# A four-layer graph network on one core: the opening loads put in order, the split of the edge network's first weight moved to 12 partitions, and some copies moved to ScalarE

## What is computed

```python
x = _layernorm(x + L0(x, src, dst, ...))              # attention over edges
x = _layernorm(x + relu((x + segment_sum(x[src], dst)) @ W))
e_h = silu(edge_attr @ edge_W1 + edge_b1)             # 53125 x 4 -> 128
e_w = sigmoid(e_h @ edge_W2 + edge_b2)                # one weight for each edge
x_agg = silu(x[src] @ agg_W + agg_b) * e_w            # L2, then update and norm
x = _layernorm(x + L3(x, edge_index, edge_type, ...))
```

## Time and profile before

| | us |
|---|---|
| median of 3 runs | 1098.27 (1097.43 to 1101.11) |
| the profiled execution: time | 1098.61 |
| the profiled execution: span | 1096.8 |
| PE busy in the span | 1009.4 (92%) |
| DVE busy | 907.4 (83%) |
| ACT busy | 722.1 (66%) |
| POOL busy | 217.8 (20%) |

### The profile page before, as it was taken

How to read it: one execution, slowest core, us unless ns; L and a number is a source line. 1 busy time by engine, 2 the same in 40 slices (tenths; PEclk the granted TensorE clock), 3 DMA queues, 4 the chain that set the end, 5 groups by cost and what they waited for, 6 DMA issues and landing times.

```text
span 1096.8 us, 28220 instructions
## 1 busy us (share of the span) xinstructions
PE 1009.4 (92%) x10463; PEld 865.8 (79%) x10463; DVE 907.4 (83%) x2226; ACT 722.1 (66%) x1559; POOL 217.8 (20%) x260
## 2 busy tenths in 40 slices
PE   3797979699999999995999999779999999989997
PEld 3343557599999999994677787759999999976765
DVE  6775999988998989988999999878787888766754
ACT  3466765555545555457899999567677776776554
POOL 4401340000000000000000000226676667610000
PEclk9899999899999999996999999889999999999999
DMA  6000020344444445410543344235444444357463
GB/s 158 1 1 1 4 68 3 110 147 149 165 128 157 157 139 168 135 64 21 168 130 128 126 124 127 75 113 141 126 142 138 121 138 133 116 188 237 145 171 116
DMA packets 79198, 128.27 MB, mean 117 GB/s; under 512 B 11147, under 2 KB 53206, under 8 KB 78828
## 3 DMA queue, kind: packets, MB, share of 16 engines
q1 hardware_dynamic: 73577, 115.20, 33.5%
q0 software_dynamic: 5056, 10.36, 3.8%
q10 hardware_dynamic: 426, 0.85, 0.3%
HBM read 101.50 MB, written 24.88 MB: 115 GB/s over the span
## 4 chain that ended last, share of the span: by engine, by line
PE 76%; DVE 12%; ACT 6%; issue 3%; DMA 1%; POOL 0%; POOLq 0%; SPq 0%; DVEq 0%; ACTq 0%
PE PS L2424 14%; PE PS L2618 14%; PE PS L2412 11%; PE PS L2601 8%; PE PS L2704 6%; PE PS L2529 5%; PE PS L2497 2%; PE PS L2250 2%; PE PS L2504 2%; PE PS L2263 2%; DVE vo L1592 2%; DVE ring L1588 2%; PE PS L2327 2%; ACT ring L1221 1%; ACT X L1160 1%
## 5 line engine op out<-in xcount | busy, mean ns | idle before, releaser
L1084 ACT CAST vo<-XT 128x768 f32<-128x768 bf16 (+1 forms) x218 | 180.3, 827 | 136.7 <-PE PS L2618 64.1
L920 POOL DMA_INDIRECT XT<-tab,ring x158 | 160.6, 1016 | 112.0 <-PE PS L2618 60.8
L2424 PE MATMUL PS<-vo 128*128 128x133 f32 x1300 | 175.9, 284 | 1.0 <-DVE vo L1694 1.0
L2424 PEld LDWEIGHTS PS<-vo 128*128 128x128 f32 x1300 | 157.2, 191 | 1.1 <-issue 1.1
L2412 PE MATMUL PS<-kp,ring 128*128 128x132 bf16 x1950 | 146.1, 220 | 3.3 <-DVE ring L1562 1.8
L2618 PE MATMUL PS<-vo 128*128 128x128 f32 x984 | 132.8, 279 | 0.0
L2412 PEld LDWEIGHTS PS<-kp,ring 128*128 128x128 bf16 x1950 | 125.3, 97 | 5.5 <-DVE ring L1562 1.9
L1570 DVE TENSOR_TENSOR XT<-iotab,XT 128x768 bf16<-128x768 bf16 (+1 forms) x218 | 119.8, 550 | 2.5 <-ACT XT L1077 2.5
L2618 PEld LDWEIGHTS PS<-vo 128*128 128x128 f32 x984 | 118.9, 191 | 3.0 <-issue 2.4
L2414 PE MATMUL PS<-SDP,ring 128*128 128x12 bf16 x650 | 110.0, 169 | 0.0
L1562 DVE TENSOR_SCALAR ring<-ring,pcolm 128x1664 bf16<-128x1664 bf16 x146 | 91.0, 651 | 19.1 <-PE PS L2601 15.5
(11 more groups left out here) (345 smaller groups left out, 2134.2 us busy)
## 6 DMA issues: line engine op xcount, KB each, us to landing
ring<-rows_d SPq DMA_DIRECT2D x146, 416.0 KB, 4.7
adj_d<-ring SPq DMA_DIRECT2D x100, 128.0 KB, 1.7
adj_d<-ring SPq DMA_DIRECT2D x75, 96.0 KB, 1.6
ring<-adj_d SPq DMA_DIRECT2D x11, 640.0 KB, 4.2
vo<-adj_d SPq DMA_DIRECT2D x9, 640.0 KB, 4.2
vo<-adj_d SPq DMA_DIRECT2D x8, 480.0 KB, 3.9
ring<-adj_d SPq DMA_DIRECT2D x7, 480.0 KB, 4.4
XT<-tab,ring POOLq DMA_INDIRECT x158
```

The lines of the kernel that those rows point to most:

```text
L920: G.indirect_dma_start(far_rows[:, f % FBUF, :], None, tab[2], bass.IndirectOffsetOnAxis(ap=far_row[:, t:t + 1], axis=0)).then_inc(far_in[ ...
L1084: C.copy(ohd[:, k % 3, 0:n, :], ohb[:, k % 3, 0:n, :]).then_inc(hots_wide, 1)
L2424: T.matmul(bank(6 + b % 2)[:, 0:VW], ohd[:, k % 3, i, :], vals[:, k % 3, i, :], start=j == 0, stop=j == JN - 1).then_inc(scattered, 1)
```

## The change

The loads of the opening are put in order by waits: the attribute loads on ScalarE's queue wait for the edge list to land (`edges_in`), and the node rows on SyncE's queue wait for the attributes (`attr_in`). `edge_W1` is loaded three times onto 12 partitions and `edge_b1` broadcast beside it (`W12`). VectorE splits these 12 x 256 numbers into three parts, choosing by partition, ahead of its wait for the edge list; TensorE's product with `S` then spreads parts that are final, and ScalarE copies the result from `bank(4)` to `We1b`. The selectors `psel` fall away, small ones in `pgrp` come. ScalarE also takes over the copy of columns 80 to 96 of `attrS`, and does one small Silu early. GpSimd clears only the spare columns of `SLc`, and makes three small iotas in place of one.

```diff
@@ -374,9 +374,13 @@
         hv = big[:, 6864:7376].rearrange("p (k f) -> p k f", k=4)
-        We1 = big[:, 6864:6864 + GE]
-        we1a = big[:, 7376:7376 + GE // 2].bitcast(bf16)
-        we1c = big[:, 7632:7632 + GE // 2].bitcast(bf16)
+        W12 = T0f[0:12, 0:2 * F]
+        W12a = T0f[0:12, 2 * F:3 * F].bitcast(bf16)
+        W12c = T0f[0:12, 3 * F:4 * F].bitcast(bf16)
+        W12p = T0f[0:12, 4 * F:6 * F]
+        S = T0f[0:12, 6 * F:10 * F].rearrange("p (u r) -> p u r", u=U)
+        code = T0f[0:12, 10 * F:10 * F + ATT]
+        pgrp = T0f[0:12, 11 * F:11 * F + 8]
         We1b = sb("We1b", [P, U * F], bf16)
@@ -384,13 +388,8 @@
...
-        S = sb("S", [4, U, P])
-        S1 = sb("S1", [1, P])
-        psel = sb("psel", [P, 3])
+        code_i = sb("code_i", [12, ATT], i32)
+        S1 = sb("S1", [3, P])
@@ -676,6 +675,7 @@
             sp.wait_ge(padded, 4)
+            sp.wait_ge(attr_in, 16 * (len(ROWS) + (REM > 0)))
             sp.dma_start(X[:, 0:HNB, :], ins["x"][0:HNB * P, :].rearrange("(b p) f -> p b f", p=P)).then_inc(x_in, 16)
@@ -823,7 +823,8 @@
             G.iota(iota_i[:, :], pattern=[[1, P]], base=0, channel_multiplier=0).then_inc(iotas, 1)
-            G.iota(m16_i[:, :], pattern=[[0, P // 16], [1, 16]], base=0, channel_multiplier=0).then_inc(iotas, 1)
+            for part, (c0, c1) in enumerate(((0, 48), (48, 80), (80, 96))):
+                G.iota(code_i[:, c0:c1], pattern=[[0, (c1 - c0) // 16], [1, 16]], base=16 * part, channel_multiplier=0).then_inc(iotas, 1)
             G.iota(pcol_i[:, :], pattern=[[0, 1]], base=0, channel_multiplier=1).then_inc(iotas, 1)
@@ -831,9 +832,9 @@
             G.memset(onesb[:, :], 1.0).then_inc(pool_consts, 1)
-            G.memset(SLc[:, :, :, :], 0.0).then_inc(pool_consts, 1)
+            G.memset(SLc[:, :, :, 4 * (NB % BANKS) + 3:BP:4], 0.0).then_inc(pool_consts, 1)
             G.memset(attrS[:, :, ATT:ATW], 1.0).then_inc(pool_consts, 1)
             G.tensor_copy(IJ[:, :], iota_i[:, 1:JN + 1]).then_inc(pool_consts, 1)
@@ -965,8 +966,10 @@
 
-            act.dma_start(eW1[:, :], ins["edge_W1"]).then_inc(we1_in, 16)
-            act.dma_start(eb1[:, :], ins["edge_b1"].rearrange("(o f) -> o f", o=1)).then_inc(we1_in, 16)
+            for part in range(3):
+                act.dma_start(W12[4 * part:4 * part + 4, 0:F], ins["edge_W1"]).then_inc(we1_in, 16)
+            act.dma_start(W12[:, F:2 * F], ins["edge_b1"].rearrange("(o f) -> o f", o=1).to_broadcast([12, F])).then_inc(we1_in, 16)
+            act.wait_ge(edges_in, 16 * 3 * (len(ROWS) + (REM > 0)))
             for n, (r0, r1) in enumerate(ROWS):
@@ -979,6 +982,8 @@
 
+            act.wait_ge(consts, 1)
+            C.activation(okr[:, :], pcol[:, :], ACT.Silu)
             for k in range(2):
@@ -989,8 +994,12 @@
             C.copy(attrS[:, :, 0:16], attrE).then_inc(part_act, 1)
+            act.wait_ge(part_act, 1)
+            C.copy(attrS[:, :, 80:96], attrS[:, :, 0:16]).then_inc(part_act, 1)
             act.wait_ge(part_dve, 1)
             C.copy(attrS[:, :, 16:32], attrE).then_inc(part_act, 1)
+            act.wait_ge(we1_mm, 1)
+            C.copy(We1b[:, :], bank(4)).then_inc(we1_ready, 1)
             def heads_copy(k):
@@ -1405,13 +1414,32 @@
             V.memset(X[:, NB - 1, :], 0.0).then_inc(padded, 1)
...
              dve.sem_inc(consts, 1)
+
+            link(V.tensor_scalar(pgrp[:, 0:1], pcol[0:12, :], 4.0, None, ALU.is_ge))
+            link(V.scalar_tensor_tensor(pgrp[:, 1:2], pcol[0:12, :], 8.0, pgrp[:, 0:1], ALU.is_ge, ALU.add))
+            loose(V.scalar_tensor_tensor(pgrp[:, 2:3], pgrp[:, 1:2], 12.0, pcol[0:12, :], ALU.mult, ALU.add))
+            for part in range(3):
+                loose(V.tensor_scalar(pgrp[:, 3 + part:4 + part], pgrp[:, 1:2], float(part), None, ALU.is_equal))
+            loose(V.tensor_copy(code, code_i[:, :]))
+            loose(V.memset(S, 0.0))
+            loose(V.memset(S1[:, :], 0.0))
+            dve.wait_ge(we1_in, 64)
+            link(V.tensor_copy(W12a, W12))
+            link(V.tensor_tensor(W12, W12, W12a, ALU.subtract))
+            link(V.tensor_copy(W12c, W12))
+            link(V.tensor_tensor(W12, W12, W12c, ALU.subtract))
+            for c0, sel in ((0, pgrp[:, 3:6]), (F, ident[0:12, 0:3])):
+                cs = slice(c0, c0 + F)
+                link(V.tensor_scalar(W12p[:, cs], W12[:, cs], sel[:, 2:3], None, ALU.mult))
+                link(V.scalar_tensor_tensor(W12p[:, cs], W12c[:, cs], sel[:, 1:2], W12p[:, cs], ALU.mult, ALU.add))
+                loose(V.scalar_tensor_tensor(W12p[:, cs], W12a[:, cs], sel[:, 0:1], W12p[:, cs], ALU.mult, ALU.add))
 
@@ -1421,16 +1449,13 @@
 
-            loose(V.memset(S[:, :, :], 0.0))
-            loose(V.memset(S1[:, :], 0.0))
             loose(V.memset(eps[:, :], LN_EPS))
-            loose(V.tensor_copy(m16[:, :], m16_i[:, :]))
             loose(V.tensor_copy(identb[:, :], ident[:, :]))
...
             settle()
-            loose(V.memset(S1[:, ATT:ATK], 1.0))
+            loose(V.tensor_copy(S1[:, ATT:ATK], ident[0:3, 0:3]))
             for u in range(U):
-                loose(V.tensor_scalar(S[:, u, 0:ATT], m16[:, 0:ATT], -4.0 * u, pcol[0:4, 0:1], ALU.add, ALU.is_equal))
+                loose(V.tensor_scalar(S[:, u, 0:ATT], code, -4.0 * u, pgrp[:, 2:3], ALU.add, ALU.is_equal))
             settle()
@@ -1452,15 +1477,8 @@
             loose(V.tensor_scalar(pcolm[:, :], pcol[:, :], -float(P), None, ALU.add))
-            for k, n in enumerate((48, 80, 96)):
-                loose(V.tensor_scalar(psel[:, k:k + 1], pcol[:, :], float(n), None, ALU.is_lt))
             settle()
-            loose(V.scalar_tensor_tensor(TRI[:, :], ident[:, :], RANK0, TRI[:, :], ALU.mult, ALU.add))
-            link(V.tensor_tensor(psel[:, 2:3], psel[:, 2:3], psel[:, 1:2], ALU.subtract))
-            link(V.tensor_tensor(psel[:, 1:2], psel[:, 1:2], psel[:, 0:1], ALU.subtract))
-            for k in range(3):
-                loose(V.scalar_tensor_tensor(psel[:, k:k + 1], pcol[:, :], float(ATT + k), psel[:, k:k + 1], ALU.is_equal, ALU.add))
-            settle()
+            link(V.scalar_tensor_tensor(TRI[:, :], ident[:, :], RANK0, TRI[:, :], ALU.mult, ALU.add))
             dve.sem_inc(consts, 1)
@@ -1509,20 +1527,9 @@
             rank_hots(0)
-            dve.wait_ge(we1_mm, 1)
-            link(V.tensor_copy(We1, bank(4)))
-            link(V.tensor_copy(we1a, We1))
-            link(V.tensor_tensor(We1, We1, we1a, ALU.subtract))
-            link(V.tensor_copy(we1c, We1))
-            link(V.tensor_tensor(We1, We1, we1c, ALU.subtract))
-            link(V.tensor_scalar(We1b[:, :], we1a, psel[:, 0:1], None, ALU.mult))
-            link(V.scalar_tensor_tensor(We1b[:, :], we1c, psel[:, 1:2], We1b[:, :], ALU.mult, ALU.add))
-            link(V.scalar_tensor_tensor(We1b[:, :], We1, psel[:, 2:3], We1b[:, :], ALU.mult, ALU.add))
-            dve.sem_inc(we1_ready, 1)
-            dve.wait_ge(part_act, 2)
+            dve.wait_ge(part_act, 3)
             dve.wait_ge(part_dve, 1)
             loose(V.tensor_copy(attrS[:, :, 48:80], attrS[:, :, 0:32]))
-            loose(V.tensor_copy(attrS[:, :, 80:96], attrS[:, :, 0:16]))
             settle()
@@ -2228,11 +2235,10 @@
             pe.wait_ge(consts, 2)
-            pe.wait_ge(we1_in, 32)
             pe.wait_ge(base_ready, 1)
             for u in range(U):
-                T.matmul(bank(4)[:, u * F:(u + 1) * F], S[:, u, :], eW1[:, :], start=True, stop=False)
-                o = T.matmul(bank(4)[:, u * F:(u + 1) * F], S1[:, :], eb1[:, :], start=False, stop=True)
+                T.matmul(bank(4)[:, u * F:(u + 1) * F], S[:, u, :], W12p[:, 0:F], start=True, stop=False)
+                o = T.matmul(bank(4)[:, u * F:(u + 1) * F], S1[:, :], W12p[0:3, F:2 * F], start=False, stop=True)
             o.then_inc(we1_mm, 1)
@@ -2310,7 +2316,7 @@
-                    pe.wait_ge(part_act, 2)
+                    pe.wait_ge(part_act, 3)
```

8 lines of the change are left out of this document (2 added, 6 removed).

## The result

The changed kernel took 1092.02 us (median of 5 runs, 1088.86 to 1094.81), against 1098.27 for the kernel before (5 runs, 1097.43 to 1101.11). The ratio is 0.9938 with an interval of 0.9913 to 0.9964: 6.2 us less, where 9.6 were forecast. The profiled execution took 1093.46 with a span of 1091.6, against 1096.8 for the span of before.

A forecast was written before the change was run, and what follows sets the result against it. TensorE bounds the kernel as a whole, but the opening waits on a load and then VectorE. Front 2.1, block 5.7 and clock 1.8 sum to 9.6: 1098.6 - 9.6 = 1089.0 us, range 1085.5 to 1094.0.

The forecast's parts named there:

- The term of the front: Opening up to the edge list's cast: cast starts at 8.8 in place of 10.93, 2.1 us earlier.
- a clock that falls anyway: Rival: remaining TensorE idle time still makes the clock fall, leaving a 7.2 us gain, 1091.4 us; chance 0.20.
- late small loads: Rival: small weight loads land late and VectorE stalls ahead of the cast, gain 6.5, 1092.1 us; chance 0.10.
- three signs of being wrong: Attributes landing after 13, clock at 0.50 behind attr_transposed(0), or mixed stage's 9.6 us gain missing at the end.
- The edge list's landing: Opening: loaded without the attributes beside it, the edge list lands near 7.0 us.
- The attributes' landing: Opening: issued after the edge list, 830 KB takes 3.5 us plus 2.2 for the way, landing at 12.7.
- The rival by late attributes: Slower: attributes loaded behind the edge list hold up their strand; decides at a landing of 22.4; chance 0.02.
- The split ahead of the cast: VectorE's weight split on 12 partitions before the edge list's cast: 3.7 us from 5.1, so the cast starts at 8.8.
- The bounds of -1.0 and 3.9: Limits on the front's 2.1 us: 3.9 if only the landing counts, -1.0 if the small loads land at 8.2.
- The work between the one-hot planes: VectorE work removed between rank_hots(0) and rank_hots(1): rank_sums(3) gains 5.7 us, between 5.1 and 6.0, limited by TensorE.
- The clock: TensorE's idle stretch before rank_sums(3) goes, so its clock no longer falls behind it: 1.8 us, up to 2.4.
- rival of a gain given back: Rival: stages behind 98 us idle and lose clock anew, 7.2 of 9.6 lost, 1096.2 us; chance 0.06.

The follow-up runs named there:

- small_loads_last: Changed kernel with the four layer L0 tensors, edge_W2 and edge_b2 loaded behind the attributes: 1089.74 us, ratio 0.992 to the kernel before.
- clears_late: Changed kernel with GpSimd's clearings behind the first one held until the edge list is cast: 1092.87 us, one run.
- no_load_waits: Changed kernel without the two waits that order the attribute and node-row loads: 1092.07 us, ratio 0.9942 to the kernel before.
- copy_back: Changed kernel with the copy of columns 80 to 96 of attrS back on VectorE, off ScalarE: 1092.71 us, one run.
- all_three: Changed kernel with six small loads behind the attributes, GpSimd's clearings held until the edge cast, and the split behind the edge list's fields: 1087.74 us, ratio 0.9899.
- no_early_silu: Changed kernel without the small early Silu on ScalarE, so the table loads at the first real Silu: 1091.24 us, one run.

## Why the prediction came out 3 us too low

**The direction and two of the three terms** were right: the idle stretch of TensorE is gone, the clock holds in the mixed stage, and all that stands before the placement moves with them. The term of the front was not. Of 9.6 us, 8.1 are there at the placement, and the 1092.0 us lie in the range, 3.0 above the forecast. That owes something to luck: the 2.9 us given back behind the placement (below) could as well have been more or less. Two rivals give such a number (1091.4 by a clock that falls anyway, 1092.1 by late small loads), but neither is what happened: the clock held, and the small loads of the weight were there when VectorE asked (4.99). Of the prediction's own three signs of being wrong, two came: the attributes landed at some 14.4, behind 13, and not all that was seen at the end of the mixed stage was there at the end. By its own terms its range would run from 1086.6 to 1093.0; it was set about 1 us wider on either side.

**The edge list's landing** was forecast at about 7.0; it was there by 6.04, when ScalarE's queue passed its wait. The attributes' landing was forecast at 12.7 and came at some 14.4, 8.4 us behind the issue. The step that failed was to take the rate of the earlier trace rows and 2.2 us for the way. Issued behind the edge list, at 6.04, the load stood among the six other loads and was slow to start; with the small loads behind it (`small_loads_last`) it had landed by 12.06. The rival by late attributes had the place right, but its point of decision, 22.4, was never near.

**The split ahead of the cast** was priced at 3.7 us for an engine that runs undisturbed, which `clears_late` confirms with 3.69. It took 5.16, since its neighbour on GpSimd was not counted. The narrow rows come from 58 us, where GpSimd does nothing; what the other engine does at the new place was not looked at. The two delays lie side by side, not one behind the other: either alone puts the attribute transposes at 14.1 to 14.5, where 12.8 was forecast. This is the term that was wrong: the cast **2.1 earlier by forecast, 0.8 measured** (10.15 against 10.96), and 0.3 of it left at the first rank sum. Some of the difference went inside `rank_hots(0)`, which takes 3.50 us from its first row to the first rank sum (22.41 to 25.91) in place of 3.18 (23.05 to 26.23). Its reason, the cheaper landing, was true and without effect: `no_load_waits` has the same front. (The issue of the attributes at 1.58, for which the prediction names, is a row of ScalarE's queue and does not stand there.) The bounds of -1.0 and 3.9 enclose the value; the small loads, though, were in time, and the price of the split by the Trainium skill ("VectorE: DVE Perf Modes", the TRN2 errata), an estimate of 2.1, is well under the undisturbed 3.69.

**The work between the one-hot planes** was priced at 5.7 within 5.1 to 6.0, and measured at 5.54. It is TensorE and ScalarE that limit it, as the prediction said; `copy_back` shows it for the copy of columns 80 to 96. That the cast of the weights on ScalarE costs nothing is read from the trace only: it ends at 24.10, long before TensorE asks. What the prediction did not have is that TensorE's first rank sums run at the lower speed for longer than before (last section): `rank_sums(2)` ends at 31.4 in spite of the earlier front, and that is worth 0.5 of this term.

**The clock** was priced at 1.8 (up to 2.4), and measured at 2.2: the mixed stage takes 67.6 in every kernel that has the early Silu and in which the clock stays at 1.00 up to 92 us, and 69.8 to 70.0 in the three in which it falls between 31 and 35 us. Where it falls matters: in `no_load_waits` and `all_three` it is at 0.50 from 93.1 and 92.3 us on, and "mixed" is 67.59 and 67.57 all the same, since at its end TensorE waits for VectorE (3.4 to 4.9 us ahead of the placement). The table load was counted at nothing, and with the early Silu it costs nothing in the mixed stage. But it lay beside `rank_hots(1)` before, and that cover is gone: without the early Silu it would cost 0.6 (`no_early_silu`).

**What came back.** 8.1 us at the placement, 6.2 by the medians and 5.2 by the two profiled spans. The prediction's rival of a gain given back is what happened in part: TensorE's clock falls once more, in the first layer, from 157.7 to 164.5. At half speed those 6.8 us are worth up to 3.4, and the pair of traces differs by 2.9 behind the placement. In the table of the clock the same code differs by up to 4.3 from kernel to kernel, with the clock and not in the order of the placement times. So it shows by how much the clock moves the rest; which moment it falls at was not controlled in any run, and stays open.

## What to carry to other kernels

Before work is moved ahead on VectorE, look at GpSimd at the new place: a row's duration from a quiet stretch is a lower bound. A wait that puts an urgent load first pays only where its reader would otherwise stand on the load: here it brought nothing with the split ahead of the cast, and 3.5 us once the split, the clearings and the small loads were out of the way; test it again after each edit of that stretch. An edit of the opening should be read where its stage ends: the untouched rest differs by 4 us between kernels here, with the clock, and that is as much as the edit.
